# Two conditioned layers on one core: the setup's weights packed in four partition groups, step 0's convolution from three contiguous copies of x, and all setup orders changed

## What is computed

```
h = gelu(cond@W0+b0); h = gelu(h@W1+b1); att = softmax(h@W2+b2)      # [128, 8]
agg_w = einsum('bk,koi->boi', att, weight); agg_b = att @ bias_k
c = einsum('boi,bih->boh', agg_w, x) + agg_b[:, :, None]
x = x + c @ (A @ B.T).T + bias                                       # rank 128
y = conv1d(x, weight[64, 16, 9], pad=4, groups=4) + cond @ c_weight.T + fside
d = argmax-routed LoRA of y (4 experts, rank 8)
x = x + y @ W_up.T + d
```

## Time and profile before

| | |
|---|---|
| time, median of 3 runs | 1109.08 us (1108.52 to 1109.31) |
| span of the profiled execution (first to last instruction) | 1106.9 us |
| time of the profiled execution itself | not recorded apart; the median less the span is 2.2 us |
| busy: PE, DVE, ACT, POOL | 1080.5, 912.0, 605.8, 4.6 us |
| granted TensorE clock, mean | 0.993 of full |

### The profile page before, as it was taken

One profiled execution on the slowest core, in us unless ns is written; L12 is line 12 of the kernel. 1 busy time (PEld: TensorE's weight loads), 2 busy tenths in 40 slices (PEclk: granted clock), 3 DMA queues, 4 the chain that ended last, 5 costly groups with the idle time before them and its releaser, 6 DMA issues.

```text
span 1106.9 us, 19141 instructions
## 1 busy us (share of the span) xinstructions
PE 1080.5 (98%) x7020; PEld 1049.8 (95%) x7020; DVE 912.0 (82%) x1670; ACT 605.8 (55%) x1243; POOL 4.6 (0%) x17
## 2 busy tenths in 40 slices
...
GB/s 342 221 133 151 136 113 122 148 155 143 136 115 112 147 152 150 134 115 121 136 150 158 128 112 123 139 145 160 130 117 114 142 142 161 133 125 92 107 58 77
DMA packets 118481, 152.03 MB, mean 137 GB/s; under 512 B 21885, under 2 KB 92285, under 8 KB 118237
## 3 DMA queue, kind: packets, MB, share of 16 engines
...
...
## 4 chain that ended last, share of the span: by engine, by line
PE 91%; DVE 4%; DMA 1%; ACT 1%; issue 1%; SPq 1%; ACTq 0%; DVEq 0%
PE M L1445 40%; PE H L1445 9%; PE G L1445 9%; PE F L1394 8%; PE F L1344 8%; PE F L1315 3%; PE F L1316 2%; PE F L1314 2%; PE M L1379 2%; PE G L1379 2%; PE M L1480 2%; SPq L355 1%; DMA Xr<-x 1%; PE F L1331 1%; PE F L1332 1%
## 5 line engine op out<-in xcount | busy, mean ns | idle before, releaser
L1445 PE MATMUL M<-Wsh,yh 128*128 128x384 f32 x896 | 308.3, 344 | 0.8 <-DVE yl L976 0.8
L1445 PE MATMUL M<-Wsl,yh 128*128 128x384 f32 x896 | 302.6, 338 | 0.0
L1445 PE MATMUL M<-Wsh,yl 128*128 128x384 f32 x896 | 302.3, 337 | 0.0
L925 DVE STREAM_TRANSPOSE yr<-F 128x512 f32<-128x512 f32 x126 | 90.2, 716 | 110.7 <-PE F L1394 110.7
L1445 PEld LDWEIGHTS M<-Wsh,yh 128*128 128x128 f32 x896 | 168.5, 188 | 4.4 <-DVE yl L976 1.1
L1445 PEld LDWEIGHTS M<-Wsl,yh 128*128 128x128 f32 x896 | 168.8, 188 | 2.7
L1445 PEld LDWEIGHTS M<-Wsh,yl 128*128 128x128 f32 x896 | 168.2, 188 | 0.0
L453 ACT ACTIVATE yh<-yr 128x1024 fp32r<-128x1024 f32 (+1 forms) x127 | 120.3, 948 | 20.1 <-DVE yr L940 14.9
L554 ACT ACTIVATE F<-G,cbX 128x128 f32<-128x128 f32 x252 | 70.4, 342 | 81.7 <-PE G L1379 81.7
L554 ACT ACTIVATE F<-M,cbX 128x128 f32<-128x128 f32 x260 | 72.6, 342 | 63.4 <-PE M L1379 63.4
L453 ACT ACTIVATE F<-biasb 128x512 f32<-128x512 f32 x124 | 74.5, 601 | 43.4 <-DVE yr L925 42.7
...
## 6 DMA issues: line engine op xcount, KB each, us to landing
...
```

Of the source, the lines that this page charges most:

```text
L925: dve.transpose(dst.rearrange("p j k m -> p (j k) m").rearrange("p (k r) (g b n) -> p g b k r n", r=2, g=2, b=4)[:, g % 2], F[g % 2][:, :] ...
L1445: last = pe.matmul(dst, w[:, y, k, :], m, start=fresh and n_ == 0, stop=k == 3 and n_ == 2, skip_group_check=True)
```

## The change

What each part does:

- `wks`: the 4096 columns are laid in four groups of partitions (32 apart, 24 used), 1024 columns each, beside the 64 of the bias. `wkr`, `wkh` and `wks` are 128 x 1088, loaded, copied and combined in two pieces of 544. GpSimd makes both copies. `ats` and `atsT` hold four copies of the 24 columns. `low` becomes a [128,1] made from two selections.
- b2 is added by a matmul of `ident` with `b2s` into the bank of h2@W2. The softmax reads that bank.
- GpSimd also makes the high parts of x for step 0 (`xTh`, two copies of 128x1024).
- Step 0's convolution has no differences. `xh0(q, h)` copies the three interleaved parts of `Xr` (even, odd, shifted even) to `Xc`, `xl0` makes the low part, `unit_c0(g)` does 12 matmuls of 256 columns, and `cbp(g)` spreads the bias alone.
- `Bh`/`Bl` and `Th`/`Tl` are split in two operations each; the buffers of xT and of the weights at the start are moved; `t1` to `t4` have semaphores of their own.
- A Gelu on a dummy (`warm`) stands near the end of ScalarE's setup list.
- All five orders ahead of the loops are new. The loops are unchanged.

```diff
+        Xc = (Xh, over("Xch1", "Wsh", [128, 3, 8, 64], 4 * BW, f32r))
+        Xe = (Xl, over("Xcl1", "Wsh", [128, 3, 8, 64], 5 * BW, f32r))
+        def parts(x, h):
+            r = x[:, 4 * h:4 * h + 4, :]
+            return bass.AP(r.tensor, r.offset, [r.ap[0], (1, 3), r.ap[1], (2, 64)])
 # sync, the order up to step 0's x
-            sp.dma_start(wkr[:, :], wkx).then_inc(d_wk, 16)
-            load_xT(0, 0); load_xT(0, 1); Br; ccs; fsB; ebb; Ar; Tr; biasb; Wcr (2)
-            w12(); w22(); load_xT(1, 1); load_xT(1, 0); x0(); load_x(1)
-            load_agg1(0..3); load_agb(1); rx0(); load_xT(2, 0); rx(0, 1); agg_out(); load_x2(2)
+            wkload(0); Br; wkload(1); Tr; load_xT0(0); ccs; load_xT0(1); Ar
+            load_xT(1, 0); fsB; load_xT(1, 1); gg(0); gg(1); w22(); w21(); agb_out(); biasb
+            load_x(1); wcl(0); load_agb(1); load_x(0); load_agg1(0); load_agg1(1); load_xT(2, 0)
+            load_agg1(2); load_agg1(3); agg_out(); rx0(); load_x2(2); load_xT(2, 1); ebb; rx1()
 # gpsimd
+            for h in range(2):
+                pool.wait_ge(d_wk[h], 16)
+                pool.tensor_copy(wkh[:, 544 * h:544 * h + 544], wkr[:, 544 * h:544 * h + 544]).then_inc(g_wk, 1)
+            for h in range(2):
+                pool.wait_ge((d_z, d_z01)[h], 16)
+                pool.tensor_copy(xh(0, h)[:, :, :], xsrc(0, h)[:, :, :]).then_inc(g_txh, 1)
             pool.wait_ge(d_cc, 16)
             pool.tensor_copy(ccX ...)
 # scalar
+            def xh0(q, h):
+                act.wait_ge(d_rx[q], 128)
+                ...
+                copy(Xc[q][:, :, 4 * h:4 * h + 4, :], parts(raw(0, q), h)).then_inc((a_x0, a_xs)[h], 1)
+            bh(0) w11() th() w12() evac(0) th2() bh(1) evac(2) evac(4) evac(5) evac(6) evac(7)
+            gg(2) gg(3) ah() ut(0) txh(1, 0) txh(1, 1) tuu(0) w(0) vhi(0) w(1) w(2)
+            bias(0, 0) bias(0, 1) bias(0, 2) bias(0, 3) wc(0) ut(1) tuu(1) bias(1, 0) txh(2, 0)
+            rx0() vhi(1) w(3) bias(1, 1) rx1() xh0(0, 0) cbp(0) cbp(1) xh0(0, 1) txh(2, 1)
+            cbp(2) xh0(1, 0) xh0(1, 1) hA(0) cbp(3) lh() ut(2) wc(1) w(4) ...
 # vector
+            (softmax) lowm() wkm(0) (ats) wkm(1) tsum() atsT tlo() blo(0) evac(1) evac(3)
+            txl(0, 0) agb_small() agb_first() txl(0, 1) blo(1) tlo2() alo() t1() cb(0)
+            txl(1, 0) csb() txl(1, 1) vv(0) t2() cb(1) cb(2) vlo(0) t3() t4() w(0)
+            addx(0, 0) addx(0, 1) wc(0) cb(3) txl(2, 0) addx(0, 2) vv(1) addx(0, 3)
+            w(1) vlo(1) w(2) w(3) xl0(0, 0) addx(1, 0) addx(1, 1) xl0(0, 1) ty(0, 0)
+            txl(2, 1) ty(0, 1) xl0(1, 0) xl0(1, 1) lA(0) ty(0, 2) llo() ty(0, 3) wc(1) ...
-            ... w(1) and w(2), w(3) of before stand behind lA(0)
 # tensor
+            def unit_c0(g):
+                q, h = g // 2, g % 2
+                pe.wait_ge(a_pc, g + 1)
+                pe.wait_ge((v_x0, v_xs)[h], q + 1)
+                ...
+                for e in range(2):
+                    for k in range(2):
+                        for n_, (w, m) in enumerate(((Th, Xc[q]), (Tl, Xc[q]), (Th, Xe[q]))):
+                            last = pe.matmul(dst[:, e], w[:, g, k, :], m[:, e + k, 4 * h:4 * h + 4, :], ...)
+            pe.matmul(M[1][:, 384:392], ident[:, :], b2s, start=True, stop=False)
+            agg_(0..7) agb_small() agb_first() u(0, 0) u(0, 1) cond() tu(0) bsum() v(0)
+            u(1, 0) u(1, 1) o(0, 0) tu(1) o(0, 1) o(0, 2) o(0, 3) v(1) u(2, 0) o(1, 0) o(1, 1)
+            c0(0) c0(1) u(2, 1) c0(2) c0(3) row(0, 0, 0) ...
-            ... agb_first() bsum() cond() u(0, 0) u(0, 1) tu(0) v(0) o(0, 0) o(0, 1) u(1, 0)
-            o(0, 2) o(0, 3) u(1, 1) tu(1) p(0, 0) p(0, 1) v(1) c(0, 0) c(0, 1) p(0, 2)
-            o(1, 0) o(1, 1) row(0, 0, 0) p(0, 3) ... c(0, 2) c(0, 3) ... u(2, 0) ... u(2, 1) ...
```

More of the change, by code:

```diff
@@ L753, in _ @@
-            pc(0, 3)
+            wc(0)
+            ut(1)
+            tuu(1)
+            bias(1, 0)
+            txh(2, 0)
+            rx0()
+            vhi(1)
+            w(3)
+            bias(1, 1)
+            rx1()
+            xh0(0, 0)
+            cbp(0)
+            cbp(1)
+            xh0(0, 1)
+            txh(2, 1)
+            cbp(2)
+            xh0(1, 0)
+            xh0(1, 1)
+            hA(0)
+            cbp(3)
+            lh()
+            ut(2)
+            wc(1)
+            w(4)
@@ L770, in _ @@
-            bias(2, 0)
-            txh(3, 0)
-            vhi(2)
-            xs(1, 1)
             bias(2, 1)
             bias(2, 2)
+            bias(2, 3)
+            ut(3)
+            xs(1, 1)
+            hA(1)
+            w(6)
             cpCD(0)
-            bias(2, 3)
-            w(6)
             pc(1, 2)
             pc(1, 3)
-            txh(3, 1)
+            warm()
+            tuu(3)
             zt(1)
-            hA(1)
-            ut(3)
             hB(1)
-            tuu(3)
@@ L1159, in _ @@
+            wkm(1)
+            tsum()
+            dve.wait_ge(p_mlp, 4)
+            dve.tensor_copy(atsT[:, :], M[0][:, 0:128]).then_inc(v_mlp, 1)
+            tlo()
+            blo(0)
             evac(1)
             evac(3)
-            blo()
             txl(0, 0)
@@ L1164, in _ @@
             agb_first()
-            tsum()
             txl(0, 1)
-            wc(0)
-            cb(0)
-            cb(1)
-            alo()
-            t3()
-            csb()
-            wc(1)
-            vv(0)
-            cb(2)
-            txl(1, 0)
-            vlo(0)
-            t1()
-            addx(0, 0)
-            txl(1, 1)
-            addx(0, 1)
-            llo()
-            t2()
+            blo(1)
+            tlo2()
+            alo()
+            t1()
+            cb(0)
@@ L1184, in _ @@
+            txl(1, 0)
+            csb()
+            txl(1, 1)
+            vv(0)
+            t2()
+            cb(1)
+            cb(2)
+            vlo(0)
+            t3()
+            t4()
+            w(0)
+            addx(0, 0)
+            addx(0, 1)
+            wc(0)
+            cb(3)
+            txl(2, 0)
             addx(0, 2)
+            vv(1)
             addx(0, 3)
-            cb(3)
-            tlo()
-            t4()
-            xd(0, 0)
-            xlr(0)
-            w(0)
@@ L1192, in _ @@
-            xld(0)
-            vv(1)
-            xd(0, 1)
-            xlr(1)
-            ty(0, 0)
-            ty(0, 1)
+            w(1)
             vlo(1)
-            txl(2, 0)
-            lA(0)
+            w(2)
+            w(3)
+            xl0(0, 0)
             addx(1, 0)
             addx(1, 1)
-            xld(1)
-            w(1)
+            xl0(0, 1)
+            ty(0, 0)
+            txl(2, 1)
+            ty(0, 1)
+            xl0(1, 0)
+            xl0(1, 1)
+            lA(0)
@@ L1205, in _ @@
             ty(0, 2)
+            llo()
             ty(0, 3)
[L1207 removed]
+            wc(1)
             S1(0)
+            xd(1, 0)
             S3(0)
[L1210 removed]
+            addx(1, 2)
             S2(0)
[L1212 removed]
+            txl(3, 0)
+            vv(2)
             S4(0)
+            xs(1, 0)
+            lC(0)
             addx(1, 3)
[L1215 to L1218 removed]
+            lB(0)
+            vlo(2)
+            zc0()
@@ L1524, in _ @@
             pe.wait_ge(a_mlp, 2)
-            pe.matmul(F[2][:, 384:392], h2, W2s, start=True, stop=True).then_inc(p_mlp, 1)
-            pe.wait_ge(g_con, 3)
-            pe.wait_ge(v_mlp, 7)
-            pe.transpose(M[0][0:24, 0:128], ats[:, :], ident[:, :]).then_inc(p_mlp, 1)
-            for c in range(8):
-                agg_(c)
+            pe.matmul(M[1][:, 384:392], h2, W2s, start=False, stop=True).then_inc(p_mlp, 1)
+            pe.wait_ge(g_con, 5)
+            pe.wait_ge(v_mlp, 5)
```

635 lines of the change are left out of this document (323 added, 312 removed).

## The result

| | median us | lowest to highest | runs |
|---|---|---|---|
| before | 1108.89 | 1108.52 to 1109.31 | 4 |
| after | 1101.61 | 1100.20 to 1103.48 | 4 |

The change makes the kernel faster: the ratio is 0.9934, 95% interval 0.9920 to 0.9948. The prediction was 1104.9 us in a range from 1102.2 to 1110.0. The sign was right; the gain is 7.3 us instead of 4.2, and the median lies 0.6 us under the range. In two later comparisons, each beside the kernel before on another chip, the changed kernel took 1101.54 and 1101.52 us.

A forecast was written before the change was run, and what follows sets the result against it. VectorE was taken to bound the setup up to `row(0, 0, 0)`. Start +0.85, matmuls -4.6 and idle -0.5 gave -4.25 us: span 1106.9 to 1102.65, time 1104.9 us, range 1102.2 to 1110.

The forecast's parts named there:

- The collision: Setup: GpSimd's two copies of x delay VectorE, priced in full at 2.06 us, 1.2 us net.
- both meet operations with two inputs from SBUF: Setup: reason for the full price, each of GpSimd's two x copies running beside a VectorE operation with two SBUF inputs.
- `csb` waited for `bsum`: Setup: VectorE, ready for `csb` at 23.4 us, waits 0.65 us until `bsum` ends at 23.85.
- The start: End of setup: `row(0, 0, 0)` starts at 55.1 us, 0.85 later than before.
- `w(1)`, `w(2)` after `t2`: Setup: ScalarE's weight copies wait for VectorE's `t2`; VectorE then waits about 1.9 us at `addx(0, 1)`.
- the way from `xl0(0, 0)` to the rows: End of setup: `xl0(0, 0)` ends at +19.3 us after `t2`, last `xl0` at 26.25, `c0(3)` and the rows at 27.7.
- Matmuls behind the start: TensorE behind `row(0, 0, 0)`: 39 fewer matmuls of 0.118 us, 4.6 us less.
- Idle behind the start: TensorE behind `row(0, 0, 0)`: about 1.4 us idle in place of 1.9, so -0.5 us.
- Rest: Whole kernel: time taken as 2.2 us above the span, 1104.9 us from a span of 1102.65.
- Rival D: Setup: cheap GpSimd copies, no wait for `bsum`, `o(0, 1)` at the higher clock; 1102.7 us. Chance 0.64 together with the forecast.
- Rival B: Setup: TensorE's low clock delays the start by 3.7 or 4.3 us; 1108.8 us, no change. Chance 0.22.
- C: Setup: the clock is low at both places, start 8.0 us later, 1112.9 us, slower. Chance 0.14.

## Why the prediction was wrong by 3.3 us

Its sum was 0.85 (start) - 4.6 (matmuls) - 0.5 (idle) = -4.25 us. Point by point, with three profiled executions after:

| step | predicted | measured |
|---|---|---|
| `atsT` copied by | 10.25 | 10.8 to 10.9 |
| VectorE at `agb` | 16.4, no wait | 15.8, waits to 16.05; 16.12; 16.02 |
| `bsum` done, `csb` | 23.85 | 23.40, 24.14, 24.40 |
| `t2` ends | 27.35 | 26.67, 27.40, 27.67 |
| from `t2` to the end of `addx(0, 1)` | 8.7 | 7.06 in all three |
| from `t2` to `xl0(0, 0)` | 18.35 | 16.66, 16.67, 16.90 |
| from `xl0(0, 0)` to the rows | 9.4 | 9.51, 10.45, 10.46 |
| start of `row(0, 0, 0)` | 55.1 | 52.84, 54.52, 55.03 |
| from there to the end | -5.1 | -7.1, -7.7, -7.7 |

**Bounds and method: right.** VectorE bounds the setup, the loop stays saturated, the joint is `row(0, 0, 0)`. All of the gain is ahead of 110 us.

**The collision: the two copies priced at 2.06 us, measured 0.8 to 1.1, and without effect.** GpSimd's first copy of x met `tlo` and `blo(0)`. It was issued while `tlo` ran and took 1.63 us instead of 1.03; then `blo(0)` took 1.52, 0.83 more than its second half alone. The second copy (13.64 to 14.68 us) met only the two evacuations from PSUM, `evac(1)` and `evac(3)`, which took 0.68 us each as ever: it cost nothing. The step that failed is "both meet operations with two inputs from SBUF". What can meet `txl(0, 0)` is the copy of `ccX`. In the first execution `txl(0, 0)` starts at 14.61, just ahead of it; it takes its usual 1.21 us and GpSimd's copy 1.67. In the third the copy comes first, takes 0.61, and VectorE pays 0.3:

```profile
14.39 0.61 POOL L481 COPY ccX<-small 128x512 f32<-128x512 f32 x1
```

```profile
14.58 1.50 DVE L882 TENSOR_TENSOR xTl<-xTr,xTh 128x1024 fp32r<-128x1024 f32 x1
```

The Trainium skill, "SBUF — State Buffer", section "SBUF: two separate sides", says that whichever of the two engines starts first holds the shared port pair for its whole instruction, and the other blocks. The trace agrees in each of these meetings, and in the kernel with three more copies, where the engines take turns (0.25, 0.83 and 0.84 us for VectorE). A meeting that was not priced stands ahead of both: beside GpSimd's copy of `wkh` (8.08 to 9.23 us) the second scaling of `ats` took 0.62 us instead of 0.24, over half of the 0.6 by which `atsT` was late. So the price of a copy lies between 0 and nearly its whole length, by which engine comes first and how much of the copy is left. The earlier arrival at `agb` (0.3 to 0.6 us) changed nothing, as `csb` waited for `bsum` anyway, as predicted.

**The start: 1.0 us too late on average.** Two errors of opposite sign. The step "`w(1)`, `w(2)` after `t2`" failed: block 2 isn't made by `t2`. VectorE had no wait at `addx(0, 1)`, and all behind it was 1.65 us earlier; the kernel with that wait put back is 1.2 to 2.0 us slower. Against it stands the way from `xl0(0, 0)` to the rows. The 9.4 us of the prediction already had `c0(0)` at the lower clock. With `c0(0)` at the lower clock, as in two of three executions, it took 10.45, and 9.51 with the higher. The prediction let the rows start 1.45 us behind the last `xl0`, with only `c0(3)` left by then. In fact `c0(2)` starts only when the last `xl0` but one is done, 24 matmuls then stand ahead of the rows, and these start 2.3 us behind it (50.58 to 52.84 us, and 52.72 to 55.03 in the third execution).

**Matmuls behind the start: 4.6 us, measured 5.3 to 5.8.** The counts are right: of the forms L1394 and L1314 to L1316 behind the joint, 252 and 240 became 248 and 232, and three `p` are gone, 39 in all. The price of 0.118 us is that of a matmul within a unit; TensorE's busy time fell by 0.7 to 1.2 us more, of which the beginnings of five units that are gone would be some 0.4 (an estimate: a first matmul takes 0.19 to 0.20 from start to start, five times 0.08 more). What else is in it is not settled.

**Idle behind the start: the term that was mis-sized most.** I had 1.4 us, from VectorE's 12.8 us to `lC(0)` against TensorE's 11. Measured: 0.24, 0.07 and 0.07 us up to 110. VectorE ends `lC` 12.0 us after the start in the first execution (64.85 us), 11.5 in the two others, and TensorE comes to `row(0, 3, 0)` about then as well, so they meet. That is 1.3 us of the miss.

**Rest.** The three executions took 1.7 to 1.8 us more than their spans (1101.73 over 1100.0, 1100.20 over 1098.4), where the sum had 2.2: 0.4. The fifteen executions of before on the last chip took 1.7 to 2.0 us more than their spans too; 2.2 came of a median that was set against the span of a faster execution.

Together: -1.0 (start), -1.3 (idle), -1.05 (work), -0.45 (time to span), which is -3.8; the three profiled executions took 1101.06 us on average, 3.8 under the forecast, and the median of the first comparison 3.3. Rival D (1102.7), which was part of the forecast, had the right direction; its reason, cheap copies and no wait for `bsum`, was not the one: `csb` waited 0.2 us for `bsum` in all three. Rival B, the clock, is real as a mechanism; its price is 1 to 2 us between executions, not 3.7 or 4.3. C did not come.

What makes the gain is then the order, and what it needs. The packed weights give VectorE some 3.7 us in the setup (four passes of 1.3 us, became two of 0.79), worth 0.9 of each us in the new order, if what was measured by adding holds for taking away, and nothing in the old; the three `w`, set into the wait for `rx0`, are worth 4.6 us or more; and the conv from three copies, by itself 1.1 us of work more, stands ahead of the rows as a whole. These prices don't add up to the 7.3 us, as each depends on the others. The new order without the packed weights was tried only by putting more than their time back, which left 1.4 us of gain; the new order with the old convolution was not tried.
